# State-space block with two layer norms: VectorE's slot order in pass A, a second scan round of 13 steps, states split in every other slot

## The reference

```
xn    = (x - mean) / sqrt(var + eps) * gamma + beta
delta = sigmoid(xn @ w_delta + b_delta)          # 16 numbers a token
B     = xn @ w_in + b_in                         # 16 numbers a token
gate  = sigmoid(xn @ w_gate + b_gate)            # 512 numbers a token
h[t]  = tanh((h[t-1] * delta[t]) @ A + B[t])     # a scan over 2048 tokens
x1    = layernorm(x + (h @ C) * gate + x)
out   = layernorm(x1 + real(ifft(fft(x1) @ w)) + bias)
```

## Time and profile before

| | us |
|---|---|
| median of 3 runs (887.3 to 888.64) | 888.32 |
| the profiled execution | 890.39 |
| its span, first to last instruction | 888.6 |
| TensorE busy | 850.6 |
| VectorE busy | 752.7 |
| GpSimd busy | 576.1 |
| ScalarE busy | 559.7 |
| mean granted TensorE clock | 0.995 |

### The profile page before, as it was taken

One profiled execution on the slowest core, in us unless ns is written; L12 is line 12 of the kernel. 1 busy time (PEld: TensorE's weight loads), 2 busy tenths in 40 slices (PEclk: granted clock), 3 DMA queues, 4 the chain that ended last, 5 costly groups with the idle time before them and its releaser, 6 DMA issues.

```text
span 888.6 us, 16580 instructions
## 1 busy us (share of the span) xinstructions
PE 850.6 (96%) x5074; PEld 455.2 (51%) x5106; DVE 752.7 (85%) x1513; ACT 559.7 (63%) x1066; POOL 576.1 (65%) x906
## 2 busy tenths in 40 slices
PE   8799999999889999999999999999999999999996
PEld 5345455454445555554555555554455555555553
DVE  7878888889999888888789999989878888888883
ACT  5244444543454445444368888888878887888887
POOL 4555556678664555656656666676767776777782
PEclk9999999999999999999999999999999999999998
DMA  8478888777656666777546565657868667767743
GB/s 307 161 267 301 312 309 316 252 268 255 233 195 225 203 204 246 261 254 248 204 150 234 194 235 190 236 195 228 252 226 282 220 237 251 243 231 235 264 163 142
DMA packets 94190, 209.53 MB, mean 236 GB/s; under 512 B 3760, under 2 KB 5040, under 8 KB 90160
## 3 DMA queue, kind: packets, MB, share of 16 engines
q1 hardware_dynamic: 93840, 208.49, 68.7%
q10 hardware_dynamic: 288, 0.27, 0.1%
HBM read 139.53 MB, written 67.11 MB: 233 GB/s over the span
## 4 chain that ended last, share of the span: by engine, by line
PE 62%; DVE 14%; issue 11%; POOL 9%; ACT 3%; DMA 1%; another core or an unknown queue 0%; POOLq 0%; DVEq 0%; ACTq 0%
PE bank L1501 16%; PE bank L1502 16%; PE bank L1504 16%; PE bank L1472 6%; POOL lo_sb L791 5%; PE bank L1657 3%; PE bank L1584 2%; DVE bn L1217 2%; DVE xs_sb L1249 2%; DVE gsum_sb L1264 2%; PE bank L1564 1%; ACT hi_sb L550 1%; DVE zh_sb L1133 1%; DMA x_sb<-x 1%; POOL a_rstd L777 1%
## 5 line engine op out<-in xcount | busy, mean ns | idle before, releaser
L791 POOL TENSOR_TENSOR lo_sb<-xs_sb,hi_sb 128x512 f16<-128x512 f32 x128 | 150.5, 1176 | 148.2 <-ACT hi_sb L550 148.2
L1501 PE MATMUL bank<-wg_hi,hi_sb 128*128 128x512 f16 x508 | 193.1, 380 | 8.4 <-DVE gsum_sb L1264 5.2
L870 POOL TENSOR_TENSOR x_sb<-x_sb,gate_sb 128x512 f32<-128x512 f32 x120 | 153.1, 1276 | 71.9 <-DMA x_sb<-x 57.6
L1501 PE MATMUL bank<-w_re_sb,hi_sb 128*128 128x512 f16 x512 | 194.0, 379 | 2.0 <-DVE w_ring L1375 1.4
L1502 PE MATMUL bank<-w_re_sb,hi_sb 128*128 128x512 f16 x512 | 194.0, 379 | 0.0
L1502 PE MATMUL bank<-wg_lo,hi_sb 128*128 128x512 f16 x508 | 192.8, 379 | 0.0
L550 ACT ACTIVATE hi_sb<-xs_sb 128x512 f16<-128x512 f32 x128 | 80.5, 629 | 168.3 <-DVE xs_sb L1249 165.3
L1504 PE MATMUL bank<-w_re_sb,lo_sb 128*128 128x512 f16 x512 | 131.4, 379 | 0.0
L1504 PE MATMUL bank<-wg_hi,lo_sb 128*128 128x512 f16 x508 | 131.2, 381 | 0.0
L1254 DVE SCALAR_TENSOR_TENSOR lo_sb<-bank,hi_sb 128x512 f16<-128x512 f32 x128 | 88.5, 692 | 49.5 <-ACT hi_sb L710 46.5
L718 ACT ACTIVATE norm_sb<-x_sb,lift_bias,rstd 128x512 f32<-128x512 f32 x128 | 103.1, 806 | 24.3 <-POOL lift_bias L883 23.7
(11 more groups left out here) (198 smaller groups left out, 1341.9 us busy)
## 6 DMA issues: line engine op xcount, KB each, us to landing
x_sb<-x SPq DMA_DIRECT2D x63, 1024.0 KB, 6.4
gate_dram<-gate_sb SPq DMA_DIRECT2D x32, 1024.0 KB, 5.2
out<-out_sb SPq DMA_DIRECT2D x31, 1024.0 KB, 5.3
gate_sb<-gate_dram SPq DMA_DIRECT2D x30, 1024.0 KB, 7.1
out_sb<-x_turned SPq DMA_DIRECT2D x16, 1024.0 KB, 7.3
norm_sb<-x_turned SPq DMA_DIRECT2D x15, 1024.0 KB, 7.3
w_ring<-gate_dram SPq DMA_DIRECT2D x2, 1024.0 KB, 9.6
x_sb<-x SPq DMA_DIRECT2D x2, 512.0 KB, 5.4
```

The lines of the kernel that those rows point to most:

```text
L791: pool.tensor_tensor(lo_sb[:, k % 4], xs_sb[:, k % 2], hi_sb[:, k % 4], ALU.subtract).then_inc(s_lo, 1)
L870: pool.tensor_tensor(x_sb[:, k // 4, k % 4], x_sb[:, k // 4, k % 4], gate_tile(n, k), ALU.add).then_inc(s_v, 1)
L1501: nc.tensor.matmul(dst, hi_sb[:, slot_of, t], w_hi[:, t], start=(t == 0), stop=False)
```

## The change

VectorE's slot in pass A gets another order: the logits of the tile just done first, then the aggregate, now of tile n + 7 (its statistics were taken at the end of the slot before), `copy_z`, `token_scale` with `token_inverse` right behind it, the scan step, `scaled(n + 2)`, `combine`, `sum_zrow`, `row_factors`, and `a_statistics(n + 8)` last before the split and the preparation steps. TensorE's spread for tiles 8 to 11 moves from its slot 5 to its slot 6. The second round of the scan ends after 13 steps, and the comparison takes the thirteenth state of each chunk in both rounds; check, branch and the first part of the split come three slots earlier. The four parts of the split are done in every other slot, so the last part stays in its slot (109 in pass A, 44 in pass B).

```diff
+SECOND = 13
+STEPS = CHUNK + SECOND
...
-SCAN_CHECK = tuple(n + 2 * CHUNK for n in SCAN_FIRST)
+SCAN_CHECK = tuple(n + STEPS for n in SCAN_FIRST)
...
-    return (j // CHUNK, j % CHUNK) if 0 <= j < 2 * CHUNK else None
+    return (j // CHUNK, j % CHUNK) if 0 <= j < STEPS else None
+
+
+def split_place(n, first):
+
+    return (n - first) // 2 if isinstance(n, int) and n - first in (0, 2, 4, 6) else None
...
-                nc.vector.tensor_copy(ends[rows], last)
+                nc.vector.tensor_copy(ends[rows], h_sb[rows, :, compared::CHUNK])
...
-                nc.vector.tensor_tensor(differ[rows], h_sb[rows, :, CHUNK - 1::CHUNK], ends[rows],
+                nc.vector.tensor_tensor(differ[rows], h_sb[rows, :, compared::CHUNK], ends[rows],
                                         ALU.not_equal).then_inc(s_dscan[g], 1)
...
-                    if s + 1 < CHUNK:
+                    if s + 1 < (CHUNK, SECOND)[r]:
                         scan_product(g, s)
                     elif r == 0:
-                        scan_next_round(g)
+                        scan_next_round(g, SECOND - 1)
                     else:
-                        scan_compare(g, 1)
+                        scan_compare(g, 1, SECOND - 1)
...
             def split_slot(g, n):
-                if isinstance(n, int) and 0 <= n - SCAN_SPLIT[g] < 4:
-                    state_low(g, n - SCAN_SPLIT[g])
+                if split_place(n, SCAN_SPLIT[g]) is not None:
+                    state_low(g, split_place(n, SCAN_SPLIT[g]))
...
-                if isinstance(n, int) and 1 <= n < 8:
-                    gate_logits(n - 1, n - 1, 0)
                 if isinstance(n, int) and n == 3:
                     projection_bias()
                 if isinstance(n, int) and n == SCAN_BRANCH[0]:
                     scan_until_settled(0)
+                if exists(n + 7) and not (isinstance(n, int) and n < 5):
+                    dve.wait_ge(s_bn, n + 8)
+                if exists(n - 1):
+                    gate_logits(n - 1, (k - 1) % 8, v if k >= 1 else v - 1)
+                if exists(n + 7) and not (isinstance(n, int) and n < 5):
+                    aggregate(n + 7, (k + 7) % 8, 8, s_aggr)
                 if k == 4 and exists(n - 8):
                     copy_z(v - 1)
                 if k % 4 == 1 and exists(n + 3):
                     token_scale(v * 2 + (k + 3) // 4, (k + 3) // 4 % 2)
+                    token_inverse((k + 3) // 4 % 2)
+                scan_slot(0, n)
                 if exists(n + 2) and not (isinstance(n, int) and n == -1):
                     scaled(n + 2, (k + 2) % 8, v if k < 6 else v + 1)
-                if k % 4 == 1 and exists(n + 3):
-                    token_inverse((k + 3) // 4 % 2)
+                if isinstance(n, int) and pair_at(n - 1) is not None:
+                    combine(pair_at(n - 1))
+                if k % 4 == 1 and exists(n - 4):
+                    sum_zrow(v if k == 5 else v - 1, 0 if k == 5 else 1)
...
                 elif exists(n + 8):
                     a_statistics(n + 8, k, v + 1)
-                    dve.wait_ge(s_bn, n + 9)
-                if exists(n - 1) and not (isinstance(n, int) and n < 8):
-                    gate_logits(n - 1, (k - 1) % 8, v if k >= 1 else v - 1)
-                if exists(n + 8) and not (isinstance(n, int) and n < 4):
-                    aggregate(n + 8, k, 8, s_aggr)
-                scan_slot(0, n)
-                if isinstance(n, int) and pair_at(n - 1) is not None:
-                    combine(pair_at(n - 1))
-                if k % 4 == 1 and exists(n - 4):
-                    sum_zrow(v if k == 5 else v - 1, 0 if k == 5 else 1)
                 split_slot(0, n)
...
-                if isinstance(n, int) and n == 2:
-                    spread_token_scale(1, 1)
-                if k % 4 == 1 and before(n, 2) and exists(n + 3):
+                if isinstance(n, int) and n in (2, 6):
+                    spread_token_scale((n + 2) // 4, (n + 2) // 4 % 2)
+                if k % 4 == 1 and before(n, 6) and exists(n + 3):
                     spread_token_scale(v * 2 + (k + 3) // 4, (k + 3) // 4 % 2)
```

More of the change, by code:

```diff
@@ L644, in scan_until_settled @@
                 with act.If(changed > 0):
-                    with act.Fori(2, LANES) as r:
+                    with act.Fori(2, LANES + 1) as r:
                         again = act.value_load(flag[g][0:1, 0:1])
@@ L648, in scan_until_settled @@
                             for s in range(CHUNK):
-                                scan_tanh(g, r * CHUNK + s + 1, s)
+                                scan_tanh(g, r * CHUNK + SECOND - CHUNK + s + 1, s)
                             act.wait_ge(s_flag[g], r)
@@ L666, in split_slot @@
             def split_slot(g, n):
-                if isinstance(n, int) and 0 <= n - SCAN_SPLIT[g] < 4:
-                    state_high(g, n - SCAN_SPLIT[g])
+                if split_place(n, SCAN_SPLIT[g]) is not None:
+                    state_high(g, split_place(n, SCAN_SPLIT[g]))
             def slot(n, k, v):
@@ L1134, in scan_product, with scan_next_round @@
                                         del_sb[rows, :, s + 1::CHUNK], ALU.mult).then_inc(s_hd[g], 1)
-            def scan_next_round(g):
+            def scan_next_round(g, compared):
                 rows = scan_rows(g)
@@ L1146, in scan_next_round, with scan_compare @@
                                         del_sb[rows, :, CHUNK::CHUNK], ALU.mult).then_inc(s_hd[g], 1)
-                nc.vector.tensor_copy(ends[rows], last)
-            def scan_compare(g, r):
+                nc.vector.tensor_copy(ends[rows], h_sb[rows, :, compared::CHUNK])
+            def scan_compare(g, r, compared):
                 rows = scan_rows(g)
-                nc.vector.tensor_tensor(differ[rows], h_sb[rows, :, CHUNK - 1::CHUNK], ends[rows],
+                nc.vector.tensor_tensor(differ[rows], h_sb[rows, :, compared::CHUNK], ends[rows],
                                         ALU.not_equal).then_inc(s_dscan[g], 1)
@@ L1166, in scan_until_settled @@
                 with dve.If(changed > 0):
-                    with dve.Fori(2, LANES) as r:
+                    with dve.Fori(2, LANES + 1) as r:
                         again = dve.value_load(flag[g][0:1, 0:1])
                         with dve.If(again > 0):
-                            scan_next_round(g)
+                            scan_next_round(g, CHUNK - 1)
                             for s in range(CHUNK):
-                                dve.wait_ge(s_h[g], r * CHUNK + s + 1)
+                                dve.wait_ge(s_h[g], r * CHUNK + SECOND - CHUNK + s + 1)
                                 if s + 1 < CHUNK:
                                     scan_product(g, s)
-                            scan_compare(g, r)
+                            scan_compare(g, r, CHUNK - 1)
                             scan_flag(g, r)
@@ L1595, in scan_until_settled @@
                 with pe.If(changed > 0):
-                    with pe.Fori(2, LANES) as r:
+                    with pe.Fori(2, LANES + 1) as r:
                         again = pe.value_load(flag[g][0:1, 0:1])
@@ L1599, in scan_until_settled @@
                             for s in range(CHUNK):
-                                scan_step(g, r * CHUNK + s + 1, s)
+                                scan_step(g, r * CHUNK + SECOND - CHUNK + s + 1, s)
                             count_changes(g, r)
```

## The result

The changed kernel takes 896.25 us (894.24 to 897.7, 4 runs) against 887.81 (886.84 to 888.64, 4 runs) before: ratio 1.0094, interval 1.0069 to 1.0119. It is slower, by 8.4 us in the medians. The two profiled executions differ by less: 894.24 us with a span of 892.4 after, 890.39 and 888.6 before.

A forecast was written before the change was run, and what follows sets the result against it. TensorE, busy 96% of the span, was taken to bound the kernel, with idle in pass A. Pass A +6.4 us and pass B -2.3 gave +4.1 on the median of 888.3: 892.4 us, range 886 to 903.

The forecast's parts named there:

- The two waits named: Pass A: VectorE's logits wait for ScalarE's sigmoid, 0.6 us a slot; TensorE's spread waits for diag, 0.43 and 1.02 us.
- the two circles: Plain round in pass A: TensorE's circle with late spreads takes 24.76 us, VectorE's with sigmoid waits 24.63, nearly equal.
- The plain round: Eight tiles of pass A without preparation: 23.3 us becomes 24.8, +1.5, with bounds 23.3 and 25.4.
- Tiles 42 to 97: Pass A: tiles 42 to 81 135.0 us against 135.1, preparation partly hidden; tiles 82 to 97 62.6, +0.6.
- Tiles 98 to 113: Pass A: three scan steps fewer (-1.5) against spread idles of 1.0 and 1.45; 55.8 us against 55.89, no change.
- Pass B: Second half, order kept: three fewer scan steps -1.3 us, spaced split -1.0, together -2.3.
- The start: Up to tile 10: the moved spread starts it at 54.9 us instead of 56.52, -1.6, unless a second idle lowers the clock.
- rival C: TensorE's clock falls with the repeated idles; half of 13 rounds affected, +10 us, 903; chance 0.07.
- A: Rival: chains bind less than counted; shortened scan and hidden preparation win, a round costs 0.9, 884.6 us; chance 0.15.
- B: Rival: it cancels, by half of A or a bigger win at start and preparation rounds, 887 to 890; chance 0.15.
- E: Rival: the thirteenth scan step still differs on chip, forcing another round, 24 us a group, 916; chance 0.04.
- D: Rival: VectorE's longer slot and tanh and pair waits add up in tiles 66 to 113, 1.5 us a round, 900; chance 0.13.

The follow-up runs named there:

- sigmoid_first: The changed kernel with ScalarE's sigmoid of tile n-2 moved ahead of its high half of tile n+2: 891.86 us, ratio 1.0028.
- stats_first: The changed kernel with GpSimd's row statistics moved ahead of its low half in slots 4j: 878.73 us, ratio 0.9891.
- stats_and_sigmoid_first: The changed kernel with both GpSimd's row statistics ahead of its low half and ScalarE's sigmoid ahead of its high half: 868.65 us, ratio 0.9773.
- split_together: The changed kernel with the four parts of each split again in four slots in a row, 13 steps kept: 897.57 us, ratio 1.0092.
- after_again: The changed kernel measured once more, unedited: 896.47 us (892.88 to 899.07, 6 runs), ratio 1.0079.
- start_only: The kernel before with only TensorE's spread for tiles 8 to 11 moved from slot 5 to slot 6: 887.35 us, ratio 0.9991.
- scan_split_only: The kernel before with only the second scan round of 13 steps and the split in every other slot: 884.66 us, ratio 0.9958.
- best: The kernel before with 13 scan steps, spaced split and moved spread, VectorE's order as before: 883.91 us, ratio 0.9947.
- order_only: The changed kernel with 16 second-round scan steps and the split in four consecutive slots, leaving VectorE's order and the moved spread: 902.04 us, ratio 1.0157.
- best_both_first: VectorE's order of before, 13 steps, spaced split, moved spread, plus GpSimd's statistics ahead of low half and ScalarE's sigmoid ahead of high half: 873.21 us, ratio 0.9824.

## Why the prediction was right, and where it missed

**Direction and main mechanism: right.** The span grew by 3.8, predicted +4.1, the loss lies in the plain rounds and the spread waits for diag in them. The two waits named are the ones found, and of its signs VectorE's wait for the mean square fell as told (32.7 to 5.8 us, about 10 predicted).

**Which of the two matters: only half told.** The prediction gave the two circles as nearly equal, 24.76 and 24.63. The runs part them. Without the sigmoid's wait a round is 24.9, without the late mean square 23.68, without either 23.1 (sigmoid_first, stats_first, stats_and_sigmoid_first). In a plain round the token chain is what costs; the sigmoid's wait adds 0.2 to it, and 0.6 once the chain is short. Over the whole kernel it is worth more: some 5 us without the other edit, 10 with it. VectorE's wait was 42.1 us, not 60; that the late spread covers the rest of it is likely and was not tested.

**The plain round: mis-sized by 0.37.** It grew by 1.88 us, from 23.29 to 25.17. TensorE's idle grew by 1.5 of that, from 0.20 to 1.70 a round, as the forecast said (0.43 and 1.02 in turn predicted, 0.55 and 1.18 measured, less the 0.2 that before idled elsewhere). The term that the sum put at nothing is TensorE's busy column: 93.88 instead of 92.35 over four rounds, 0.38 a round. In a stream a small product of 0.18 us starts 0.03 behind the one before it (a large one of 0.38 starts 0.22 behind); at each stall that overlap of 0.15 is lost, twice a round. The remaining 0.1 is of the record: the window of before lacks its eight spread products (x650 against x658). An idle of TensorE costs the idle and some 0.15.

**Tiles 42 to 97: right in kind, 2.7 too long** (194.9 against 197.6 predicted). The preparation steps do hide in the new order, a little more than counted. Of the 2.7, 0.3 is a slip: the terms given for tiles 82 to 97 (59.69, twice 1.0, 0.6) add up to 62.3, not 62.6.

**Tiles 98 to 113: missed, +1.6.** The prediction counted VectorE's split as work only. Timeline of after:

```profile
386.81 0.68 DVE L1189 SCALAR_TENSOR_TENSOR h_lo<-h_sb,h_hi 64x512 f16<-64x512 f32 x1 [1.85 <-ACT h_hi L663]
...
393.84 0.39 PE L1435 MATMUL bank<-diag,ones_b 128*128 128x512 bf16 x1 [2.58 <-POOL diag L793]
```

The high and low part are ScalarE's and VectorE's halves of the split. The low part stands ahead of the next logits and waits 1.85 us for ScalarE's high part; two slots later the spread is 2.58 late. split_together shows that it isn't the spacing: it too has a 2.50 there. That the 1.85 makes the 2.58 is read from the order of the rows; no run takes the split's wait away alone.

**Pass B: -3.5, not -2.3.** Three steps of 0.44 give the 1.3 predicted. The split, put at 1.0, gives nothing that can be told (split_together). Another 1.1 comes from the steps that stay: before, tiles 14 to 20 took 26.51 us with stalls at 16 and 20, now 25.77, and tile 36 took 4.06 where a tile with a step takes 3.68. With smaller pieces the first 37 tiles are 2.7 shorter together; the remaining 0.7 lies behind tile 48, and its cause is open. VectorE's product in the scan became shorter, which fits the stalls that are gone; that is the last section's matter.

**The start: right in the trace, nothing in the median.** Tile 10 started at 55.41 (54.9 predicted), behind the 2 us of idle foreseen. The prediction called its loss "up to 1.6", if the second idle lowers the clock; after_again shows it do so, for 1.4, the first execution doesn't.

**The median: 3.9 above the forecast of 892.4, inside its range.** The step that missed is the carrying over of a difference between profiled executions to the medians. The profile of before was a long one (890.39 against medians of 887.8 to 889.0), with a fall of the clock at tile 6 that the change takes away. The profile of after is the one of six without the fall near 250, and has the shortest time of its four. An estimate: the spans differ by 3.8; the missing fall is 2.7 us in five of six executions, so 2.2; and if before's usual execution has no fall at tile 6, the 1.9 us that the profile gained in the start weren't there to gain. Together 7.9 of the 8.4 measured. The last condition is open. For it: start_only gains nothing in its median, and scan_split_only, with the start of before, idles the same 2.45 us there and keeps its clock; against it, that same trace has a fall at 29 us instead, at the same price (its tile 10 starts 38.6 us behind its first product, as in before, and 36.7 in start_only and best):

```profile
29.50:32.50 3.00, 3.00 (x8) 1.03 (x7) 1.02 (x3) 0.20 (x1) 1.85 (x2) 0.50 1.08 398
44.00:46.00 2.00, 1.51 (x7) 0.85 (x9) 1.97 (x6) 0.51 (x2) 1.41 (x2) 1.00 0.44 167
```

So this much of rival C is true: single idles of two and three us lower the clock in many executions. The mechanism that C told of, falls from the repeated idles, isn't: with 0.55 and 1.18 in every plain round the clock stayed at 1.00 there in both executions.

**A, B and E** didn't come, and D hardly. There was no further round of the scan: TensorE's scan products are 116 in the profile after, two for each of 58 steps. D had tiles 66 to 113 longer than forecast by 1.5 a round: 66 to 97 are 3.4 shorter than forecast, 98 to 113 longer by 0.8 a round.

## What to carry to other kernels

When one engine's order is changed, read the other engines' queues for what now has its input early and still stands behind something late: here a change that cost 8 us became 20 us faster than before by moving one block on GpSimd and one line on ScalarE. Follow the wait of the bounding engine back instruction by instruction and ask at each step on a queue whether it needs the one ahead of it; a wait of 40 us on another engine can be worth 5 us, and 10 once the wait that covered it is gone. Try edits of two queues together as well as one by one: the order that lost 12 us without them won 4.6 when both other queues followed it. And compare medians with medians: two profiled executions of a kernel here differ by 4.9 us, and three falls of the clock account for that.

## What the runs showed of the hardware that was not expected

**The same idle lowers the clock or doesn't.** Behind 2.88 us of idle before tile 70 TensorE stayed at its upper level, 2.4 GHz (1.00), in one execution of the change and fell to the lower, 1.2 GHz (0.50 from 251.0 to 253.5 us, price 2.7 us), in the other. A count at five places over the traces: an idle of 1.94 to 1.96 us before tile 2 stands in all 14, and 4 have the lower clock behind it; 2.45 before tile 6 in two, one has it; 2.04 to 2.29 before tile 10 in five, two have it; 2.4 to 3.1 near tile 70 in six, five have it; 2.4 to 3.3 near tile 110 in the same six, one has it (order_only, the 3.3). The idles of 0.55 and 1.18 in turn, one every 12 us or so, never had it. But two short ones close together did once, 1.03 and 0.87 us before the products at 218.16 and 219.42 of best_both_first:

```profile
220.50:223.50 3.00, 3.00 (x9) 1.08 (x8) 2.93 (x9) 1.01 (x3) 2.80 (x3) 0.50 0.37 150
```

The Trainium skill, "TensorE: Matmul & The Clock Gate", "A second HAM failure mode", warns of short idles between groups of products. The plain rounds here don't show that, the pair in best_both_first may be a case of it.

**A VectorE instruction takes over three times as long beside GpSimd.** The scan's product has one shape all through pass B (64x128, both inputs from SBUF). Timeline of before, its rows and those of GpSimd's large product:

```profile
492.35 1.28 POOL L870 TENSOR_TENSOR x_sb<-x_sb,gate_sb 128x512 f32<-128x512 f32 x1 [0.41 <-DVE gate_sb L1364]
493.56 0.40 DVE L1133 TENSOR_TENSOR zh_sb<-h_sb,del_sb 64x128 f32<-64x128 f32 x1
...
500.68 1.27 POOL L870 TENSOR_TENSOR x_sb<-x_sb,gate_sb 128x512 f32<-128x512 f32 x1 [1.69 <-DMA x_sb<-x]
500.73 1.45 DVE L1133 TENSOR_TENSOR zh_sb<-h_sb,del_sb 64x128 f32<-64x128 f32 x1 [0.16 <-ACT h_sb L637]
```

Started as GpSimd ends it takes 0.40; started 0.05 behind GpSimd's start it takes 1.45 and ends 0.23 after GpSimd's instruction. All 20 of the 30 that took over 0.6 us ended 0.24 to 0.27 after GpSimd's product. The groups by line over pass B's scan, before and after:

```profile
L1133 DVE TENSOR_TENSOR zh_sb<-h_sb,del_sb 64x128 f32<-64x128 f32 x30 | 25.7, 856 | 3.8 <-ACT h_sb L637 2.6
```

```profile
L1140 DVE TENSOR_TENSOR zh_sb<-h_sb,del_sb 64x128 f32<-64x128 f32 x27 | 18.5, 684 | 5.9 <-ACT h_sb L644 5.2
```

With three products fewer, 7.2 us less: the mean fell from 856 to 684 ns, and 14 of 27 are over 0.6 us long instead of 20 of 30. The Trainium skill, "SBUF — State Buffer", "SBUF: two separate sides", says that a VectorE instruction with two SBUF inputs and a GpSimd instruction that reads SBUF exclude each other for the whole instruction; the rows agree. Why 13 steps move the products out of GpSimd's way and 16 don't (order_only and start_only have 21 and 19 long ones) stays open.
